# Context blocks turned on VectorE instead of TensorE in a cross-attention and FFN kernel, with the first batch in another order

## What is computed

```python
q = layernorm(x)
s = where(mask, -1e9, einsum('bqd,bkd->bqk', q, ctx) / sqrt(512))
a = softmax(s) @ ctx                                # (8, 512, 512)
x = x + einsum('bdl,ol->bdo', swapaxes(a), W_merge) + b_merge
h = layernorm(x); hq = quant(h)                     # one scale for all of h
g = silu(hq @ quant(w_gate).T) * (hq @ quant(w_up).T)
x = x + quant(g) @ quant(w_down).T                  # one scale for all of g
```

## Time and profile before

| | |
|---|---|
| median of 3 runs | 579.25 us |
| profiled execution | 579.35 us, of which the span is 577.6 us |
| TensorE busy | 543.1 us, 94% of the span |
| VectorE busy | 454.3 us, 79% |
| ScalarE busy | 296.1 us, 51% |
| GpSimd busy | 148.8 us, 26% |
| DMA queue of SyncE | 42.8% of 16 engines |

### The profile page before, as it was taken

One profiled execution on the slowest core, in us unless ns is written; L12 is line 12 of the kernel. 1 busy time (PEld: TensorE's weight loads), 2 busy tenths in 40 slices (PEclk: granted clock), 3 DMA queues, 4 the chain that ended last, 5 costly groups with the idle time before them and its releaser, 6 DMA issues. The chain is left out here.

```text
span 577.6 us, 7625 instructions
## 1 busy us (share of the span) xinstructions
PE 543.1 (94%) x2610; PEld 359.9 (62%) x2610; DVE 454.3 (79%) x839; ACT 296.1 (51%) x431; POOL 148.8 (26%) x77
## 2 busy tenths in 40 slices
PE   6759999999999999999999499999999999699996
PEld 4547888888888888888888244444444444244442
DVE  5279889887988988889686557878777877599884
ACT  3356465545645556355431357556645743777520
POOL 1707454636545365463421000000000000000000
PEclk9969999999999999999999699999999999899999
DMA  8520535454354443441229513272060000779783
GB/s 306 184 74 1 133 136 183 136 189 88 119 174 128 170 124 121 165 134 74 48 112 150 186 73 170 104 273 73 12 260 0 0 0 2 269 269 396 244 288 153
DMA packets 47583, 82.59 MB, mean 143 GB/s; under 512 B 20416, under 2 KB 24512, under 8 KB 44992
## 3 DMA queue, kind: packets, MB, share of 16 engines
q1 hardware_dynamic: 47552, 82.20, 42.8%
HBM read 52.43 MB, written 25.43 MB: 135 GB/s over the span
## 5 line engine op out<-in xcount | busy, mean ns | idle before, releaser
L1176 PE MATMUL gu<-hid,gu_T 128*128 128x512 f16 x704 | 155.6, 383 | 0.8 <-DVE hid L1093 0.8
L1176 PEld LDWEIGHTS gu<-hid,gu_T 128*128 128x128 f16 x704 | 68.9, 99 | 84.1 <-issue 3.3
L1074 DVE SCALAR_TENSOR_TENSOR hid<-gu,gu_mul,hid 128x512 f32 (+1 forms) x88 | 65.2, 747 | 41.0 <-PE gu L1176 35.7
L996 ACT ACTIVATE hid<-gu,gu_mul 128x512 f32<-128x512 f32 x88 | 59.8, 686 | 70.4 <-PE gu L1176 64.9
L1210 PE MATMUL gu<-wd_T,gu_T 128*128 128x512 f16 x264 | 59.1, 385 | 5.0 <-DVE gu_T L1118 5.0
L546 DVE SCALAR_TENSOR_TENSOR p_lo<-probs,rinv,p_hi 128x512 fp32r<-128x512 f32 x32 | 39.8, 1243 | 21.4 <-ACT p_hi L386 21.0
L750 PE MATMUL mm<-cT_hi,qT_hi 128*128 128x512 f32 x128 | 51.2, 400 | 5.6 <-DVE qT_lo L484 5.6
L1022 ACT ACTIVATE h<-hid,inv 128x512 int8<-128x512 f32 (+3 forms) x32 | 44.2, 1456 | 17.9 <-DVE gu_T L1118 14.1
L1082 DVE TENSOR_REDUCE hmax<-hid 128x1 f32 (+2 forms) x48 | 53.1, 1119 | 0.0
L750 PE MATMUL mm<-wm_hi,p_hi 128*128 128x512 f32 x128 | 53.0, 414 | 0.0
L379 ACT ACTIVATE probs<-probs,nmax 128x512 f32<-128x512 f32 x32 | 23.2, 724 | 56.7 <-DVE nmax L537 56.7
(11 more groups left out here) (123 smaller groups left out, 958.6 us busy)
## 6 DMA issues: line engine op xcount, KB each, us to landing
h_dram<-hid SPq DMA_DIRECT2D x3, 2816.0 KB, 12.9
hid<-h_dram SPq DMA_DIRECT2D x3, 2816.0 KB, 14.0
cx<-in_ctx_dram SPq DMA_DIRECT2D x7, 1024.0 KB, 7.5
x<-in_x_dram SPq DMA_DIRECT2D x5, 1024.0 KB, 5.3
x_dram<-x SPq DMA_DIRECT2D x20, 256.0 KB, 2.4
xq<-x_dram SPq DMA_DIRECT2D x5, 1024.0 KB, 5.9
x<-x_dram SPq DMA_DIRECT2D x5, 1024.0 KB, 6.4
hid<-x_dram SPq DMA_DIRECT2D x4, 1024.0 KB, 6.5
```

Of the source, the lines that this page charges most:

```text
L996: nc.scalar.activation(silu[SILU_AT[i]], gu[2 * (i % 3)][:], ACT.Silu, scale=gu_mul[:, 0, i:i + 1]).then_inc(silu_done, 1)
L1074: nc.vector.scalar_tensor_tensor(hid[:, b % SLOTS, i * L:(i + 1) * L], gu[2 * (i % 3) + 1][:], gu_mul[:, 1, i:i + 1], silu[SILU_AT[i]], AL ...
L1176: last = nc.tensor.matmul(gu[2 * (i % 3) + g][:], gu_T[:, g, h, i * P:(i + 1) * P], xT[p][:, h, :], start=h == 0, stop=h == T - 1)
```

## The change

Batches 1 to 7: the context is no longer turned by TensorE. SyncE loads it a second time, into a new buffer `cb`, with four DMAs per batch whose runs in DRAM are 32 fp32 values (128 bytes) long; each 32x32 block then stands where it belongs in the turned matrix, and only its inside is still unturned. VectorE turns the insides in place with four 128x512 `transpose` operations (`turn_c`), ScalarE makes the high part from SBUF (`turned_hi`) and GpSimd the low part (`turned_lo`, four operations of 128x512). The 28 operations of VectorE that made low parts of turned context from PSUM go, four per batch. The plain context has one buffer now, and its next load waits for `make_c_lo` of the batch before.

Batch 0: the first query tile is turned right after the first context tile; query tiles 1 to 3 are turned in the middle of the previous group of `scores`, in other PSUM banks; the mask is made tile by tile, the statistics in three pieces, and the low part of the probabilities is made one tile later on VectorE, so that it doesn't wait for ScalarE. The tiles of W_merge are turned as 1, 1, 2 after the first three groups.

FFN, batches 1 to 7: the rounded rows are turned by four DMA transposes of SyncE instead of sixteen TensorE transposes, and ScalarE's two copies go.

```diff
+                    def load_cb(n):
+                        blocks = context[n].rearrange("(k j) (h a i) -> a j h k i", j=BLK, a=P // BLK, i=BLK)
+                        for a in range(P // BLK):
+                            sp.dma_start(cb[a * BLK:(a + 1) * BLK, :, :].rearrange("j h (k i) -> j h k i", i=BLK),
+                                         blocks[a]).then_inc(cb_in, 16)
...
-                    load_c(1)
+                    load_cb(1)
                     load_x(1)
...
                             load_x(n + 2)
+                            sp.wait_ge(cT_ready, T * (n + 1))
+                            load_cb(n + 2)
+                        if n < B - 1:
                             sp.wait_ge(c_ready, n + 1)
-                            load_c(n + 2)
+                            load_c(n + 1)
...
+                    def turned_lo(n):
+                        for h in range(T):
+                            gp.wait_ge(cT_hid, T * (n - 1) + h + 1)
+                            nc.gpsimd.tensor_tensor(cT_lo[:, h, :], cb[:, h, :], cT_hi[:, h, :].bitcast(F32),
+                                                    ALU.subtract).then_inc(cT_ready, 1)
...
                             make_rstd1(n + 1)
+                            if n == 0:
+                                turned_lo(n + 1)
                             make_mneg(n + 1)
+                            if n:
+                                turned_lo(n + 1)
                         make_c_lo(n)
...
+                    def turned_hi(n, h):
+                        act.wait_ge(cb_turned, T * (n - 1) + h + 1)
+                        if h == 0:
+                            act.wait_ge(s_done, T * n)
+                        nc.scalar.activation(cT_hi[:, h, :], cb[:, h, :], ACT.Copy).then_inc(cT_hid, 1)
...
+                    def turn_c(n, h):
+                        if h == 0:
+                            dve.wait_ge(cb_in, 64 * n)
+                        nc.vector.transpose(cb[:, h, :], cb[:, h, :]).then_inc(cb_turned, 1)
...
                                 if t < 3 and not last:
                                     row_stats1(n + 1, 2 * t - 2, 2 * t)
+                                if t == 3 and not last:
+                                    for k in range(T // 2):
+                                        turn_c(n + 1, k)
                                 probs_lo(n, t - 1)
...
                             if not last:
                                 row_bias1(n + 1)
+                                for k in range(T // 2, T):
+                                    turn_c(n + 1, k)
                             probs_lo(n, T - 1)
                             for k in range(T):
-                                if not last:
-                                    transposed_lo(n + 1, k)
                                 add_residual(n - 1, k)
...
+                        if n and k == 0:
+                            pe.wait_ge(cT_ready, T * n)
+                        product(mm[k], qT_hi, qT_lo, cT_hi, cT_lo, k, s_done,
+                                turn=T + k + 1 if n == 0 and k < T - 1 else None)
...
                         for k in range(T):
-                            if not last:
-                                transposes(n + 1, k)
                             if not start:
                                 merged(n - 1, k)
...
+                        sp.wait_ge(ints, 2 * (n + 1))
+                        for t in range(T):
+                            sp.dma_start_transpose(xT[n % 2][:, :, t * P:(t + 1) * P], xi[:, t, :]).then_inc(xT_in[n % 2], 16)
...
                         for i in range(NI):
                             gate_up(b, p, i)
-                            if i == 6 and not static(b, B - 1):
-                                turn(b + 1, 1 - p)
```

More of the change, by code:

```diff
@@ L97, in attention @@
                 xs = [xq, x1, sb("x2", [P, T, D], F32)]
-                cx = [sb(f"cx{i}", [P, T, D], F32) for i in range(2)]
+                cx = sb("cx", [P, T, D], F32)
+                cb = sb("cb", [P, T, L], F32)
                 qn = sb("qn", [P, T, D], F32)
@@ L352, in _ @@
                     nc.gpsimd.tensor_copy(ident16[:], ident[:]).then_inc(consts, 1)
-                    make_rstd1(0)
-                    make_mneg(0)
+                    first_rstd(0)
+                    first_rstd(1)
+                    first_mneg(0)
+                    first_rstd(2)
+                    for t in range(1, T):
+                        first_mneg(t)
                     for n in range(B):
@@ L454, in _ @@
                             for k in range(T):
-                                transposed_hi(n + 1, k)
-                                if not start:
-                                    norm1(n + 1, k)
-                        if start:
-                            for t in range(T):
-                                norm1(n + 1, t)
+                                turned_hi(n + 1, k)
+                                norm1(n + 1, k)
                         context_hi(n)
@@ L785, in _ @@
                     pe.wait_ge(consts, 4)
-                    for g in range(T):
+                    for g in FIRST_TURNS[:T + 1]:
                         transposes(0, g)
@@ L1009, in step @@
                                 layer_norm(b + 1, 1 - p)
-                            if i == 8 and not last:
-                                take_xT(b + 1, 1 - p)
                     steps(act, step, 1)
@@ L1064, in quantise @@
                             dve.wait_ge(affine, T if static(b, 0) else T * b + (half + 1) * T // 2)
[L1065 to L1066 removed]
+                        if static(b, 1):
+                            dve.wait_ge(turned, 2)
+                        elif not static(b, 0):
+                            dve.wait_ge(xT_in[1 - p], times(b, 2 - p, 64) - 64 * p)
                         nc.vector.tensor_copy(xi[:, part, :], y8[:, part, :]).then_inc(ints, 1)
```

216 lines of the change are left out of this document (119 added, 97 removed).

## The result

The changed kernel takes 554.59 us (median of 4 runs, 553.54 to 556.40), the kernel before beside it 579.22 us (578.79 to 579.32): a ratio of 0.958 (95% interval 0.955 to 0.961), 24.6 us less. The forecast was 553.0 in a range of 546 to 567. The execution profiled took 553.71 us, its span is 551.9.

The account below looks back on a forecast made before the run. TensorE's queue was taken to bound the kernel, except in batch 0. FFN 6.2 + steady attention steps 10.9 + start 9.5 = 26.6 us off a span of 577.6 gave 551.0, a time of 553, range 546 to 567.

Parts of the forecast that it names:

- FFN, 6.2 us: FFN, batches 1 to 7: seven TensorE turns of the next batch's rows go, 7 x 0.89 = 6.2 us, the DMA transposes hidden.
- Steady steps, 1.81 us each: Attention steps 1 to 6: four groups of context transposes leave TensorE, 4 x 0.45 = 1.81 us a step, 10.9 in all.
- VectorE's transpose, 0.6 us: Turning the context blocks: each 128x512 transpose on VectorE taken as 0.6 us, by the nearer row, with none showing this operation.
- VectorE's room: Steady attention steps: the first residual, only 0.5 us later, still frees a bank for `mixed` in time, by 0.6 us.
- the other dates: VectorE's other deadlines in a step: more room; the mixed matrix's low part ends at 199.43, less 1.9, wanted at 200.3.
- VectorE becomes the bound: Rival, attention steps: first residual 1 to 2 us late per step, 6 to 12 back, 559 to 565; 0.25 with the start's.
- 4.6 to 6.2 us of low parts: GpSimd's four added low-part operations per batch: 4 x 1.16 up to 4 x 1.56 us, its step going from 18.7 to 24.
- Small packets: Context block loads: 8192 packets of 128 bytes a batch at 18 ns, 9.2 us, fit the queue; rival that they bind, 0.13.
- The loop t + 19.5: DMA queue and GpSimd between block loads: t is the blocks' time; 29 us at t = 9.2, the bound at 15.2.
- The start, 9.5 us: Batch 0 and batch 1's start: batch 1's scores at 46.5 instead of 56.03, a gain of 9.5 us, 3 either way.
- the rival on the start: Bias rows wait for vectors behind the blocks, or batch 0's chain stays long: 5 to 8 us missing, 558 to 561; 0.25 with VectorE's.
- Step 1, 1.81 us: Second attention step: counted like steps 2 to 6, 1.81 us shorter, at 34.65 us.

## Why the prediction was right, and where it wasn't

**FFN, 6.2 us.** Right. Seven turns of 0.89 us went, 6.34 in the profile; 5.4 and, by difference, 4.9 us in the timed runs (559.50 - 554.6). The rest of the profile's difference is the down projection's first tile, 17.21 against 15.85 us. It follows a wait of 5.0 us that both kernels have, and the clock comes back at a different time: a window over its first 4.5 us has 0.68 in before and 0.50 in after. Over all profiled executions the tile took 15.7 to 17.3 us. The step that failed is that it was counted at nothing; what sets the moment at which the clock comes back was not found.

**Steady steps, 1.81 us each.** Right: 36.48 to 34.56, 1.92 each, by the 0.45 us per group of the earlier trace rows. The mis-size is small: a group cost 0.48 us, not 0.45. The FFN and these steps, 15.9 of the profile's 25.7 us, are plain arithmetic from a queue that had no gap.

**VectorE's transpose, 0.6 us.** Right: 0.60 us from start to start in pairs, 0.68 alone; it was placed by the maximum's rate.

**VectorE's room.** The size was about right and the place and reason were not. The prediction had 0.6 us at the first residual. In the changed kernel the residual starts 17.1 to 21.3 us into a step instead of the 20.5 of the earlier trace rows, with need near 22. The mask, now behind the blocks on SP's queue, makes GpSimd's mask operation later, and in steps 2 to 6 it misses the third probability tile, whose 2.85 us become 0.75. (In step 6 it meets the fourth instead, for 3.73.) So the added load bought room that the prediction had not counted: 0.8 to 5 us here. With the mask ahead that tile is 2.85 us again, the residual starts 19.2 to 20.3 us into the step, and the steps stay 34.56. The step's other date on VectorE, the first `g_lo`, has 1.0 to 5.2 us, 1.0 to 1.2 in half of the steps. The prediction named "the other dates" as having more room (2.8 us by its figures), and this is the one that the run with the low part on VectorE overran, for 13.4 us. That is above the 6 to 12 that the rival "VectorE becomes the bound" had been given, through the 5.2 us ahead of batch 1's scores and the slower matmuls after some of the waits.

**GpSimd.** The size was right, the mechanism was not. 4.6 to 6.2 us of low parts were counted, 5.05 to 5.5 measured. The prediction took VectorE to be slowed, not shut out, because the tile ended before the mask operation did. The regular ends above speak against that: beside GpSimd's subtraction VectorE's operation ends a fixed time after it, beside the mask operation a fixed 1.19 us before it, whenever it began. An operation that was merely slower would end later the later it began. Nor do both have to read two SBUF operands, as the prediction put it: the mask operation reads one, and the cast that was held back reads one. SBUF — State Buffer of the Trainium skill, section "SBUF: two separate sides", has the exclusive lock for the whole instruction. Beside the subtraction the trace agrees. Beside the mask operation it agrees in that VectorE gets nothing done for a while, but not in how long: by the rule the tile at 63.31 could not have ended before 67.6, and it ended at 66.43. What GpSimd does in the rest of that operation, no run here shows.

**Small packets.** 18 ns and 9.2 us were taken; 14 to 18 ns and 7.2 to 9 us came out, under the mask's 24.6 ns of the earlier trace rows, so a smaller packet was never dearer. That the loop had room was right: rows of 2048 bytes give the same time. The loop t + 19.5 is real, and closer than it was put: at t of 7.2 to 9 us it should turn in 27 to 28.5 us, and in the changed kernel the turn from 184.35 to 213.08 took 28.7, but the one before it 37.2, with a mask that landed 9.9 us after its issue. That it would be what binds was not shown; with more packets, SP's issue time and a weight load behind it in the same loop made the waits that were followed up. DMA: Bandwidth & Descriptors of the Trainium skill (section "Specifications") asks for 512 bytes and more; runs of 128 lost rate (about 145 GB/s in the window above against 333 in the earlier trace rows), as it says, but all of it lay beside other work.

**The start, 9.5 us.** Right in kind, mis-sized by 1.9 in this execution: `mixed(0)` at 29.71 against a forecast of 30 to 31.5, batch 1's scores at 44.64 instead of 46.5. The profiled execution happened to be the quickest: seven others with the same start have 45.4 to 48.0, and the mean of all eight is 46.2, close to the forecast. The first scores, at 11.3 to 11.9 us, run at 0.23 us per matmul in this one from the second on, and at 0.42 to 0.43 for 2 to 6 us in others. The median of the runs, 554.6, sits 0.9 above this execution. The "2 us of waiting" for batch 1's queries was 0.33; the bias rows on GpSimd did wait 7.9 us for the vectors behind the blocks, as the rival on the start had it, and were still in time: with plain rows they began at 20.87 instead of 26.64, and batch 1's scores no earlier (46.01).

**Step 1, 1.81 us.** Wrong. It was treated as one of six like steps. It is the one where VectorE comes late: it works out the clip factors at the end of step 0 (2.65 and 1.01 us for two operations on 2 columns, the first held back until GpSimd's subtraction ends), starts on batch 1's scores 8.8 us after TensorE did, and meets the mask with the third probability tile at its longest. TensorE then waits 1.8 to 2.5 us for the next queries (1.1 with plain rows, 1.6 with the mask ahead). The prediction counted that wait in no step; in the kernel before, step 1 has none. Moving the factors and the mask gives most of it back.

## What to carry to other kernels

Work taken out of a queue that is busy in the whole step is gained one for one, as long as the engines that take it over keep their dates; for each such engine find every date that the busy queue depends on (here the first residual and the first low part of G) and its room, since a wait there costs itself and may cost nearly as much again in TensorE's clock. When an operation of VectorE meets one of GpSimd, count from GpSimd's end and not from a slower rate. Look separately at the first pass of a loop, where one-time work lies. Small DMA runs are cheap while the queue has room, but count the time to issue them, and what is queued behind.

## What the runs showed that was not expected

- A TensorE wait of 2 to 4 us can be paid nearly twice, or not. 2.75 us were followed by seven matmuls at 0.40 to 0.60 us instead of 0.23 (granted clock 0.64 over 4.3 us, +1.65 us), 2.05 by +1.6 us of busy time; but 2.55 us at 234.61 (low part on VectorE) and 2.15 at 277.07 (transposes three times) by a step at clock 1.00 with nothing added.
- 128-byte packets took 14 to 18 ns on an engine and 64-byte ones some 9 to 11 (estimate above), so a packet went on getting cheaper down to that size, though not in step with its bytes. The issue on SP: 5.5 to 11.6 us for 8192 packets, 10.5 to 15.8 for 16384.
- A VectorE operation that meets one of GpSimd can take two to five times as long: 2.50 to 3.99 us for a tile of 0.75 alone, 3.81 for a cast of 1.22, 5.0 for four subtractions that need 2.35. In each of these its end stands at a fixed distance from the end of GpSimd's operation: 1.19 us before the mask operation's, 1.08 and 2.35 us after the fp32 subtraction's. Not every meeting costs: the cast of 1.22 us at 52.27 lies beside GpSimd's four bias additions (51.05 to 57.14).
- Transposes of 128x512 fp32 in 32x32 blocks: 0.60 us on VectorE, 0.70 when each waits for the one before it by a semaphore.
